# A transformer block on one core: expert biases kept in SBUF, the ends of both attentions reordered, table and result additions moved, unread projections added

## The chip, the cores and the metric

One core of a Trainium2 chip runs the whole program. The metric is the device time of one execution in microseconds (us), median of several. Before the change it is 1199.89 us (three runs, 1197.47 to 1200.57).

## The reference, cut to what matters

`x` has 16 x 256 tokens of width 128. Four residual parts follow each other, each with its layer norm ahead of it:

```python
x = x + attn_a(layernorm(x), ...)   # 16 heads, q/k/v mapped to latents of 32, rope on q and k, causal softmax
x = x + ffn(layernorm(x), ...)      # 8 experts, the best 2 of each token
x = x + attn_b(layernorm(x), ...)   # 16 heads of 8, causal softmax
x = x + ffn(layernorm(x), ...)      # the same experts again

def ffn(x):                         # flat: 4096 tokens
    logits = flat @ gate_w + gate_b
    topv, topi = top_k(logits, 2); topw = softmax(topv)
    out_e = gelu(flat @ w1[e] + b1[e]) @ w2[e] + b2[e]
    return sum over e of out_e * routing weight of e
```

## The kernel before, in words

All engines run one hand-written program each and meet by semaphores; nothing is reordered by a scheduler. The residual `X` (32 tiles of 128 tokens) stays in SBUF. Each attention goes over 8 chunks of 512 tokens, and each chunk over 8 units (two batch rows by four head groups), so 64 units. A table (`PlanA`, `Plan`) gives each unit a step or two of other work for bank 7 of PSUM: projections of the next chunk (`query`, `key`, `value`), and the closing of the chunk before (`turn`, `out_t`, `out`, `gate_t`, `gate`). What is left after unit 63 is `LAST`, here called the epilogue: it closes chunks 6 and 7 and, through `first_tiles`, starts on the first tiles of the experts.

In attention b a unit is a loop between two engines. TensorE turns the row maxima (L1744), VectorE joins them to the queries (`q_aug`, L1260), TensorE makes the scores of the next unit (L1905, L1908), VectorE takes their maxima (L954, L955). TensorE makes the unit's early projection (L1662 to L1664) while it waits for the join; in the last chunk there is no next chunk, so no early projection.

The expert stage routes 8192 pairs of token and expert into 39 tiles of 256 slots (`TILES`). The first half of the tokens is ranked and placed while the attention still runs. The second half is known only after the last gate, so the routing of it (`route_second`) runs on VectorE within the first tiles: ranks, slots, the one-hot factors `lane_hot` and `block_hot`, and then at tile `TABLE_AT` TensorE multiplies these into the table of which token stands in which slot (`tokens_of`, L1687), VectorE turns it into row numbers (`sources`), and sets `slots_ready` to 2. Tiles 0 to 8 (`EARLY` is 9) are gathered from the first table; from tile 9 on GpSimd's indirect DMAs (L621) wait for `slots_ready` 2. SyncE's load of the weights of tile 9 waits for it too, and behind that load in SyncE's queue stand the stores of results.

One tile i of the loop: TensorE turns the gathered rows of tile i+2 (`turn_rows`, L1767), makes the first product of tile i+1 (`up`, L1662 to L1664, 12 matmuls) and the second product of tile i (`down`, L1983, 16 matmuls). ScalarE copies the high half of the rows (L1436) and applies Gelu. VectorE makes the low half (`split_rows`, L1167) and adds the bias `b2` (`finish`, L1311). SyncE stores the result and loads weights four tiles ahead. `b2_rows`, 512 KB, is loaded anew before each expert stage by SyncE, after the attention has let go of its memory (`attended`), and VectorE waits for it (`bias_ready`) ahead of tile 2.

The results of finished tiles come back to tokens by other indirect DMAs (`got`, L730), 16 rings deep; VectorE adds them to X (L1376). A call adds one of 64 rows ("result"); the first 32 (`RESULTS`) need only tiles below 23. In the loop they are added three per tile from tile 28 on (`ADDED_AT`). In the first expert stage GpSimd gathers results 0 to 15, makes the root for chunk 0 of attention b, gathers 16 to 23, makes the root for chunk 1, gathers 24 to 31, and goes on to attention b. The other 32 results are added in attention b's chunks 1 to 6, and at the very end after the second stage.

## Time and profile before

| | |
|---|---|
| median of three runs | 1199.89 us |
| the profiled execution | 1191.1 us, its span 1189.4 us |
| TensorE busy | 1024.3 us (86%) |
| VectorE, ScalarE, GpSimd busy | 747.3, 648.2, 758.7 us |
| mean granted TensorE clock | 0.908 |

Stages in the profiled execution: attention a to 442, its epilogue and the first tiles to 477, expert stage 1 to 616.8, attention b to 963, its epilogue and first tiles to 1002, expert stage 2 to 1139, the last 32 results to 1184. A row of the timeline gives the start, the length, the engine, the line, what is written and read, and in brackets how long the engine sat idle before it and what released it. TensorE in attention a is close to full; the idle times are in the two epilogues, at the seams of the stages and at a few places in the expert stages.

### The profile page before, as it was taken

To read this page: it belongs to the slowest core of one execution; us is meant where nothing else is said; L and a number is where in the kernel's file an instruction comes from. 1 tells how busy PE (TensorE), PEld (TensorE's weight loads), DVE (VectorE), ACT (ScalarE), POOL (GpSimd) and SP (SyncE) were. 2 spreads that over 40 slices of the span, in tenths; PEclk is the share of its full clock that TensorE was granted. 3 is DMA by queue.
4 is the path that set the end of the run, shared out by engine and by line. 5 is a ranking of instruction groups with operands and counts; after the bars stand their busy time and mean duration, and the time that the engine had idled before them with its cause. 6 is when DMAs were issued, how large, how long until landed. Compare 5 with 4: busy or idle time off the path is not lost. (4 is left out here: it accounts for less than half of the span.)

```text
span 1189.4 us, 29763 instructions
## 1 busy us (share of the span) xinstructions
PE 1024.3 (86%) x11227; PEld 793.5 (67%) x11227; DVE 747.3 (63%) x1845; ACT 648.2 (55%) x1193; POOL 758.7 (64%) x824
## 2 busy tenths in 40 slices
PE   4799999999988987999877899999988878999820
PEld 3566776676765666999874556666655557999820
DVE  5878888888889954622345677777777626322332
ACT  1476777776755543455445667767755424455410
POOL 2788988888876746277663477667534233577765
PEclk9799999999998897999997999999988658999975
DMA  9100011010000023578940000000000024688732
GB/s 263 4 2 20 19 38 37 20 37 16 6 11 2 11 72 93 162 232 251 217 121 1 1 15 24 25 16 23 13 8 4 10 98 133 182 239 222 241 104 68
DMA packets 69805, 91.10 MB, mean 77 GB/s; under 512 B 15074, under 2 KB 49762, under 8 KB 69666
## 3 DMA queue, kind: packets, MB, share of 16 engines
q1 hardware_dynamic: 58226, 68.98, 18.4%
q0 software_dynamic: 9088, 18.63, 7.3%
q8 instruction: 93, 1.52, 0.6%
q10 hardware_dynamic: 2352, 1.58, 0.5%
q14 instruction: 46, 0.38, 0.1%
HBM read 68.45 MB, written 20.71 MB: 75 GB/s over the span
## 5 line engine op out<-in xcount | busy, mean ns | idle before, releaser
L1417 ACT ACTIVATE PT<-PS 128x768 f32<-128x768 f32 x256 | 207.1, 809 | 133.0 <-PE PS L1925 79.2
L608 POOL TENSOR_SCALAR_AFFINE_SELECT PT<-PT 128x512 f32<-128x512 f32 x256 | 179.4, 701 | 144.1 <-ACT PT L1417 143.5
L621 POOL DMA_INDIRECT xg<-normed,source x156 | 148.0, 949 | 94.8 <-DVE source L1101 48.1
L1448 ACT ACTIVATE hid<-PS,b_cols 128x256 f32<-128x256 f32 x312 | 122.5, 475 | 113.3 <-PE PS L1664 110.5
L1983 PE MATMUL PS<-W,hid 128*128 x1248 | 158.9, 283 | 0.1
L1983 PEld LDWEIGHTS PS<-W,hid 128*128 128x128 f32 x1248 | 152.6, 199 | 0.6 <-issue 0.5
L730 POOL DMA_INDIRECT got<-expert_rows,slot_of x128 | 122.7, 959 | 40.2 <-issue 34.4
L1311 DVE TENSOR_TENSOR y_rows<-PS,b_rows 128x256 f32<-128x256 f32 x78 | 33.1, 425 | 149.0 <-PE PS L1983 144.1
L1755 PE MATMUL PS<-PT,v_aug 128*32 128x256 f32 (+1 forms) x2048 | 117.9, 352 | 2.2 <-POOL PT L608 2.1
L1737 PE MATMUL PS<-causal_b,ident_b 128*128 128x256 bf16 x512 | 104.1, 287 | 13.5 <-DVE q_aug L1260 12.9
L1662 PE MATMUL PS<-xg_hi,w_ring 128*128 128x256 f32 x312 | 96.9, 311 | 16.7 <-DVE xg_lo L1167 13.0
L648 POOL TENSOR_TENSOR straight<-whole,C 128x512 f32<-128x512 f32 x64 | 83.7, 1308 | 14.5 <-ACT whole L1481 14.1
L1664 PE MATMUL PS<-xg_lo,w_ring 128*128 128x256 f32 x312 | 89.7, 288 | 0.0
L1663 PE MATMUL PS<-xg_hi,w_ring 128*128 128x256 f32 x312 | 89.7, 288 | 0.0
L963 DVE TENSOR_REDUCE M<-PS 128x2 f32<-128x512 f32 x128 | 87.1, 680 | 0.0
L1755 PEld LDWEIGHTS PS<-PT,v_aug 128*32 128x32 f32 x2048 | 56.0, 114 | 41.9 <-issue 11.3
L1744 PE MATMUL PS<-C,M 128*128 128x128 f32 x256 | 58.6, 312 | 26.6 <-DVE M L963 15.0
L962 DVE TENSOR_REDUCE M<-PS 128x2 f32<-128x256 f32 x128 | 54.0, 421 | 41.0 <-PE PS L1829 40.2
L1737 PEld LDWEIGHTS PS<-causal_b,ident_b 128*128 128x128 bf16 x512 | 41.4, 101 | 54.8 <-DVE q_aug L1260 29.0
L1376 DVE SCALAR_TENSOR_TENSOR X<-got,weight,X 128x128 f32<-128x128 f32 x128 | 45.6, 366 | 51.2 <-DMA got<-expert_rows,slot_of 49.5
L955 DVE TENSOR_REDUCE M<-PS 128x4 f32<-128x1024 f32 x64 | 77.8, 1215 | 0.0
L1662 PEld LDWEIGHTS PS<-xg_hi,w_ring 128*128 128x128 f32 x312 | 61.4, 197 | 18.8 <-DVE xg_lo L1167 15.1
(301 smaller groups left out, 2993.2 us busy)
## 6 DMA issues: line engine op xcount, KB each, us to landing
w_ring<-halves_w SPq DMA_DIRECT2D x78, 512.0 KB
expert_rows<-y_rows SPq DMA_DIRECT2D x78, 128.0 KB, 3.1
normed<-xn SPq DMA_DIRECT2D x16, 256.0 KB, 2.3
xg<-normed,source POOLq DMA_INDIRECT x156
W<-in_L_ffn_w_dram SPq DMA_DIRECT2D x1, 2048.0 KB, 13.8
halves_w<-w_hi SPq DMA_DIRECT2D x8, 256.0 KB, 2.3
halves_w<-W SPq DMA_DIRECT2D x8, 256.0 KB, 2.0
got<-expert_rows,slot_of POOLq DMA_INDIRECT x128, 2.7
```

The lines of the kernel that those rows point to most:

```text
L608: nc.gpsimd.affine_select(out=diagonals, in_=diagonals, pattern=[[0, 4], [1, P]], compare_op=ALU.is_ge, fill=0.0, base=0, channel_multipli ...
L621: nc.gpsimd.indirect_dma_start(out=xg[:, i % AHEAD, b_, :], out_offset=None, in_=normed if i >= EARLY else normed[0:NH * P, :], in_offset= ...
L730: nc.gpsimd.indirect_dma_start(out=got[:, at, :], out_offset=None, in_=rows_out if c >= RESULTS // (2 * CT) else rows_out[0:FIRST_DONE * R ...
L963: ins = v.tensor_reduce(M[:, 1, cols], PS[:, banks, P:3 * P], AX, ALU.max, negate=True)
L1417: s.activation(PT[:, unit % 2, pair, :, :, :], PS[:, 4:6, 0:3 * P].rearrange("p h (a q) -> p a h q", q=P), ACT.Exp).then_inc(m["exp_done"], 1)
L1448: ins = s.activation(hid[:, r % 2, k, :], h_bank[r % 2][k // 2][:, k % 2 * ROWS:(k % 2 + 1) * ROWS], ACT.Gelu, bias=b1_cols[:, bass.ds(e * ...
L1662: t_.matmul(o, w_hi, x_hi, start=start, stop=False, skip_group_check=True)
L1663: t_.matmul(o, w_lo, x_hi, start=False, stop=False, skip_group_check=True)
L1664: return t_.matmul(o, w_hi, x_lo, start=False, stop=True, skip_group_check=True)
L1737: t_.matmul(diagonal, ident_b[:, :], causal_b[:, :].unsqueeze(1).broadcast_to([P, 2, P]), start=True, stop=False, skip_group_check=True)
L1755: ins = t_.matmul(bank[6][j * L:(j + 1) * L, at + kb * P:at + S], v_aug[:, unit // UNITS % 2, 2 * b_ + kb, g * G + j, :], PT[:, unit % 2, ...
L1983: ins = t_.matmul(y_bank[r % 2][:, b_ * P:(b_ + 1) * P], hid[:, r % 2, k, b_ * P:(b_ + 1) * P], W2[:, bass.ds(e * F + k * D, D)], start=(k ...
```

## The change

Seven edits. The names of the parts are used in the prediction.

1. **Bias.** `b2_rows` gets memory of its own, is loaded once at the start behind the expert weights, and `attended` and `bias_ready` go.
2. **Epilogues.** `out_t` and `out` of chunk 7 now come ahead of `gate` of chunk 6, in both attentions. Tile 0 is turned after `out_t`, tile 1 after that `gate`, and tile 0's first product follows. ScalarE normalizes chunk 7 ahead of Gelu of tile 0.
3. **First tiles.** Tile 1's first product comes after tile 2's turn, tile 2's first product ahead of the ranks; `split_rows` of tile 2 moves into the last choice of experts.
4. **Table.** `TABLE_AT` is 6 instead of 5; the second table covers only blocks 18 to 77 (60 instead of 78 columns); its first 16 matmuls stand ahead of tile 6's second product, its last 16 behind it.
5. **Results.** They are added from tile 32 on, three per tile; the 11 left over (21 to 31) are added in the first four units of attention b, or after the loop in stage 2. The statistics of chunks 0 and 1 move from tiles 31 and 34 to tiles 34 and 37, and ScalarE normalizes chunk 0 one tile earlier.
6. **Unread projections.** In each unit of the last chunk of attention b TensorE makes a projection (three matmuls of 512 columns) into bank 7 that nobody reads.
7. Waits on `got_used` at units 2 and 6 of attention b.

The end of attention a and the first tiles, TensorE, before (L1712 is `turn`, L1698 `gate_t`, L1767 the turn of gathered rows, L1730 `gate`, L1716 `out_t`, L1720 `out`):

```order
L1712 MATMUL PS<-C,o_t 128x128 x4
L1698 MATMUL PS<-C,xn 128x128 x4
L1767 MATMUL PS<-C,xg 128x128 x2
L1730 MATMUL PS<-gate,gate_in 128x8 x4
L1716 MATMUL PS<-C,Y 128x128 x4
L1767 MATMUL PS<-C,xg 128x128 x2
L1720 MATMUL PS<-a_out_w,y_t 128x128 x4
L1662 MATMUL PS<-xg_hi,w_ring 128x256
```

And now:

```order
L1722 MATMUL PS<-C,o_t 128x128 x4
L1708 MATMUL PS<-C,xn 128x128 x4
L1726 MATMUL PS<-C,Y 128x128 x4
L1778 MATMUL PS<-C,xg 128x128 x2
L1730 MATMUL PS<-a_out_w,y_t 128x128 x4
L1741 MATMUL PS<-gate,gate_in 128x8 x4
L1778 MATMUL PS<-C,xg 128x128 x2
L1672 MATMUL PS<-xg_hi,w_ring 128x256
```

`out_t` (now L1726) moved ahead of tile 0's turn, and `gate` behind `out`.

The table in the expert loop, TensorE, before: it stands between tile 6's first product and tile 5's second (L1687, 78 columns):

```order
L1664 MATMUL PS<-xg_lo,w_ring 128x256
L1687 MATMUL PS<-block_hot,lane_hot 128x78 x32
L1974 TENSOR_LOAD expert_of
...
L1983 MATMUL PS<-W,hid 128x128 x5
L1767 MATMUL PS<-C,xg 128x128 x2
L1662 MATMUL PS<-xg_hi,w_ring 128x256
```

And now, between tile 7's first product and the turn of tile 9 (L1778):

```order
L1674 MATMUL PS<-xg_lo,w_ring 128x256
L1697 MATMUL PS<-block_hot,lane_hot 128x60 x16
L1991 TENSOR_LOAD expert_of
...
L2000 MATMUL PS<-W,hid 128x128 x5
L1697 MATMUL PS<-block_hot,lane_hot 128x60 x16
L1778 MATMUL PS<-C,xg 128x128 x2
```

The turn of tile 9 stood two second products, a turn and a first product behind the table; now it is the next instruction.

VectorE at the start of attention b's units, now (L1385 adds results, L1264 is the join, L954 and L955 the maxima); before, the four rows of L1385 were not there:

```order
L1264 TENSOR_TENSOR q_aug<-PS,qs 128x256
L918 SCALAR_TENSOR_TENSOR qs<-PS,b_bias,minus 128x512
L954 TENSOR_REDUCE M<-PS 128x4
L955 TENSOR_REDUCE M<-PS 128x4
L1385 SCALAR_TENSOR_TENSOR X<-got,weight,X 128x128 x3
L1264 TENSOR_TENSOR q_aug<-PS,qs 128x256
```

Each addition stands between the maxima of one unit and the join of the next. The diff, cut:

```diff
@@ -38,10 +38,10 @@
 FIRST_BLOCKS = FIRST_DONE * RB
-ADDED_AT = FIRST_DONE + 5
+ADDED_AT = FIRST_DONE + 9
 ADDS = 3
 RESULTS = 8 * CT
-TABLE_AT = 5
+TABLE_AT = 6
 SPLIT_AT = UNITS
@@ -161,7 +161,7 @@
     FIRST_CLOSE = [None, None, ("prep", 0, 1), None, ("value", 0, 1), None, ("prep", 0, 2), ("turn", 0, 0)]
-    LAST = [("turn", 1, 0, 7), ("gate_t", 0, -1, 0), ("gate", 0, -1, 1), ("out_t", 0, 0, 2), ("out", 0, 0, 3), ("gate_t", 0, 0, 4), ("gate", 0, 0, 5)]
+    LAST = [("turn", 1, 0, 7), ("gate_t", 0, -1, 0), ("out_t", 0, 0, 2), ("out", 0, 0, 3), ("gate", 0, -1, 1), ("gate_t", 0, 0, 4), ("gate", 0, 0, 5)]
@@ -295,8 +296,10 @@
     k = ADDS * (i - ADDED_AT)
-    end = RESULTS if i == TILES - 1 else min(k + ADDS, RESULTS)
-    return range(k, end) if i >= ADDED_AT else range(0)
+    return range(k, k + ADDS) if i >= ADDED_AT else range(0)
+ADDED = ADDS * (TILES - ADDED_AT)
@@ -531,6 +534,7 @@
             sp.dma_start(W2[:, :].rearrange("p (e k d) -> p e k d", e=E, k=FT), w2.rearrange("e (k p) d -> p e k d", p=P)).then_inc(experts_loaded, 16)
+            sp.dma_start(b2_rows[:, :, :].rearrange("p e d -> p (e d)"), b2.rearrange("e d -> (e d)").partition_broadcast(P)).then_inc(bias_loaded, 16)
             with nc.allow_non_contiguous_dma(reason="biases as columns"):
@@ -570,10 +574,6 @@
                     keep(c, gate_norm_b(c))
-                sp.wait_ge(attended[n], 1)
-                sp.dma_start(b2_rows[:, :, :].rearrange("p e d -> p (e d)"), b2.rearrange("e d -> (e d)").partition_broadcast(P)).then_inc(me["bias_ready"], 16)
@@ -1177,11 +1180,12 @@
                     closing(m, w, s, n == "a")
-                    if s.kind == "gate" and s.c == NCH - 2:
-                        split_rows(me, 0)
                     if s.kind == "out":
                         statistics(m, NCH - 1, 1 if n == "b" else 0)
+                    if s.kind == "gate" and s.c == NCH - 2:
+                        dve.wait_ge(m["freed_dve"], s.freed)
+                        split_rows(me, 0)
                         split_rows(me, 1)
@@ -1189,8 +1193,8 @@
                             choose(part, NT - CT, NT, me)
-                v.memset(scratch1[:, :], 0.0).then_inc(attended[n], 1)
-                dve.wait_ge(attended[n], 1)
+                            if part == 0:
+                                split_rows(me, 2)
@@ -1280,8 +1284,13 @@
                     if c == 0:
+                        if adds_at(unit):
+                            add_results("1", adds_at(unit))
                         if u == 2:
+                            dve.wait_ge(moe_sems["1"]["got_used"], 6 * CT)
                             statistics(m, 2)
+                        if u == 6:
+                            dve.wait_ge(moe_sems["1"]["got_used"], RESULTS)
                         if u == 7:
@@ -1349,13 +1358,13 @@
                     add_results(n, adds_in(i))
-                    if n == "1" and i == ADDED_AT + 3:
+                    if n == "1" and i == ADDED_AT + 2:
                         dve.wait_ge(m["got_used"], 2 * CT)
                         statistics(att_sems["b"], 0)
-                    if n == "1" and i == ADDED_AT + 6:
+                    if n == "1" and i == ADDED_AT + 5:
                         dve.wait_ge(m["got_used"], 4 * CT)
                         statistics(att_sems["b"], 1, 1)
-                dve.wait_ge(m["got_used"], RESULTS)
+                dve.wait_ge(m["got_used"], ADDED)
                 weigh(1, m)
@@ -1462,9 +1472,9 @@
                 s.activation(scratch3[:, :], C[0:1, 0:1], ACT.Gelu)
+                normal(n, st.c, gate_norm_b(st.c), st.c, range(CT), 1 if n == "b" else 0)
                 act.wait_ge(b1_loaded, 16)
                 gelu(me, 0)
-                normal(n, st.c, gate_norm_b(st.c), st.c, range(CT), 1 if n == "b" else 0)
@@ -1680,12 +1690,12 @@
-            def tokens_of(h, at):
-                for k in range(2):
-                    for t in range(NH):
-                        ins = t_.matmul(at, lane_hot[:, k, :, t], block_hot[:, k, 0:BLOCKS if h else FIRST_BLOCKS, t], start=(k + t == 0),
-                                        stop=(k == 1 and t == NH - 1), skip_group_check=True)
+            def tokens_of(h, at, k, tiles=range(NH)):
+                blocks = slice(EARLY * RB, BLOCKS) if h else slice(0, FIRST_BLOCKS)
+                for t in tiles:
+                    ins = t_.matmul(at, lane_hot[:, k, :, t], block_hot[:, k, blocks, t], start=(k + t == 0),
+                                    stop=(k == 1 and t == NH - 1), skip_group_check=True)
                 return ins
@@ -1782,15 +1793,13 @@
-                if (s.kind, s.c) == ("gate_t", NCH - 2):
+                if s.kind == "out_t":
                     pe.wait_ge(m["slots_ready"], 1)
                     turn_rows(m, 0)
-                elif s.kind == "out_t":
+                elif (s.kind, s.c) == ("gate", NCH - 2):
                     turn_rows(m, 1)
-                elif s.kind == "out":
                     pe.wait_ge(experts_loaded, 32)
                     up(m, 0)
-                    up(m, 1)
@@ -1932,6 +1941,12 @@
+                def unread(last):
+                    pe.wait_ge(m["freed_act" if last.by_act else "freed_dve"], last.freed)
+                    product(bank[7], w["hi"][0][:, 0:P], w["lo"][0][:, 0:P], x_hi[:, 1, :], x_lo[:, 1, :])
                 causal(range(4))
@@ -1946,6 +1961,8 @@
                         step(plan.early[unit])
+                    elif unit >= end - UNITS:
+                        unread(next(s for u in range(unit - 1, 0, -1) for s in (plan.extra[u], plan.late[u], plan.early[u]) if s))
                     if unit + 1 < end:
@@ -1984,21 +2001,29 @@
+                table = y_bank[(TABLE_AT + 1) % 2][:, EARLY * RB:BLOCKS]
                 for i in range(TILES):
                         turn_rows(m, i + 2)
-                    if 0 < i < TILES - 1:
+                    if i == 0:
+                        up(m, 1)
+                        down(0)
+                        up(m, 2)
+                        pe.wait_ge(m["mask_ready"], 2)
+                        ranks(1, y_bank[1]).then_inc(m["rank_ready"], 1)
+                        continue
+                    if 1 < i < TILES - 1:
                         up(m, i + 1)
                         pe.wait_ge(m["y_ready"], i)
-                        tokens_of(1, y_bank[(i + 1) % 2][:, 0:BLOCKS]).then_inc(m["table_ready"], 1)
+                        tokens_of(1, table, 0)
                     if i == TABLE_AT + 1:
                     down(i)
-                    if i == 0:
-                        pe.wait_ge(m["mask_ready"], 2)
-                        ranks(1, y_bank[1]).then_inc(m["rank_ready"], 1)
+                    if i == TABLE_AT:
+                        pe.wait_ge(m["hots_ready"], 3)
+                        tokens_of(1, table, 1).then_inc(m["table_ready"], 1)
```

## Rows read from the trace of the kernel before

**Rows 1.** Part 2 of the page: granted clock in 40 slices
```profile
PEclk9799999999998897999997999999988658999975
```

**Rows 2.** Timeline of VectorE, both epilogues: start, length, what, idle before and releaser
```profile
472.26 0.42 DVE L1167 TENSOR_TENSOR xg_lo<-PS,xg_hi 128x256 fp32r<-128x256 f32 x1 [3.82 <-issue]
995.67 0.42 DVE L1167 TENSOR_TENSOR xg_lo<-PS,xg_hi 128x256 fp32r<-128x256 f32 x1 [4.07 <-issue]
```

**Rows 3.** The same, queue of SyncE (issues; length is until the queue takes them)
```profile
468.50 0.35 SPq L576 DMA_DIRECT2D b_rows<-in_L_ffn_b_dram  x1
```

**Rows 4.** The same, TensorE, first tiles of both expert stages
```profile
472.73 0.38 PE L1662 MATMUL PS<-xg_hi,w_ring 128*128 128x256 f32 x1 [3.21 <-DVE xg_lo L1167]
477.74 0.36 PE L1662 MATMUL PS<-xg_hi,w_ring 128*128 128x256 f32 x1
973.84 0.66 PE L1767 MATMUL PS<-C,xg 128*128 128x128 f32 x2 [3.78 <-DMA xg<-normed,source]
996.15 0.58 PE L1662 MATMUL PS<-xg_hi,w_ring 128*128 128x256 f32 x1 [3.30 <-DVE xg_lo L1167]
```

**Rows 5.** Table of tokens, to the first row gathered by it: TensorE, GpSimd, TensorE
```profile
955.54 3.15 PE L1687 MATMUL PS<-block_hot,lane_hot 128*128 128x46 f16 x32
489.88 5.00 PE L1687 MATMUL PS<-block_hot,lane_hot 128*128 128x78 f16 x32
496.63 0.95 POOL L621 DMA_INDIRECT xg<-normed,source  x1 [23.69 <-DVE source L1101]
497.88 0.95 POOL L621 DMA_INDIRECT xg<-normed,source  x1 [0.31 <-issue]
501.74 0.44 PE L1767 MATMUL PS<-C,xg 128*128 128x128 f32 x2 [0.54 <-DMA xg<-normed,source]
1025.80 0.38 PE L1767 MATMUL PS<-C,xg 128*128 128x128 f32 x2
```

**Rows 6.** Waits within the expert stages: TensorE
```profile
580.79 0.35 PE L1662 MATMUL PS<-xg_hi,w_ring 128*128 128x256 f32 x1 [3.51 <-issue]
608.00 0.39 PE L1662 MATMUL PS<-xg_hi,w_ring 128*128 128x256 f32 x1 [1.78 <-DVE xg_lo L1167]
1107.93 0.55 PE L1662 MATMUL PS<-xg_hi,w_ring 128*128 128x256 f32 x1 [3.24 <-DVE xg_lo L1167]
```

**Rows 7.** What VectorE waited for there
```profile
583.16 0.35 DVE L1376 SCALAR_TENSOR_TENSOR X<-got,weight,X 128x128 f32<-128x128 f32 x1 [5.46 <-DMA got<-expert_rows,slot_of]
1105.12 0.35 DVE L1376 SCALAR_TENSOR_TENSOR X<-got,weight,X 128x128 f32<-128x128 f32 x1 [3.42 <-DMA got<-expert_rows,slot_of]
```

**Rows 8.** Between expert stage 1 and attention b: TensorE, VectorE, GpSimd
```profile
612.75 4.05 PE L1983 MATMUL PS<-W,hid 128*128 x32
607.46 0.16 DVE L792 TENSOR_SCALAR var_eps<-mv 128x4 f32<-128x4 f32 x1
609.19 1.02 POOL L730 DMA_INDIRECT got<-expert_rows,slot_of  x1 [0.16 <-DVE X L1376]
621.93 0.69 DVE L904 TENSOR_TENSOR x_lo<-PS,x_hi 128x512 fp32r<-128x512 f32 x1
627.17 1.26 POOL L697 TENSOR_TENSOR ks<-whole,minus 128x512 fp32r<-128x512 f32 x1 [8.20 <-ACT minus L1556]
```

**Rows 9.** TensorE, unit 2 of attention b
```profile
653.74 0.39 PE L1737 MATMUL PS<-causal_b,ident_b 128*128 128x256 bf16 x2 [0.77 <-DVE q_aug L1260]
```

**Rows 10.** Windows: length, busy (count) by engine, granted clock, DMA share, GB/s
```profile
868.00:909.00 41.00, 35.71 (x348) 24.08 (x348) 29.11 (x69) 22.27 (x34) 15.35 (x20) 0.88 0.03 8
912.00:940.00 28.00, 25.08 (x199) 14.86 (x200) 18.31 (x39) 10.18 (x17) 9.83 (x13) 0.53 0.04 11
948.00:960.00 12.00, 9.89 (x87) 7.84 (x88) 5.71 (x16) 2.44 (x3) 1.91 (x3) 0.62 0.01 2
580.00:584.00 4.00, 3.21 (x28) 3.24 (x29) 0.65 (x2) 1.43 (x4) 2.92 (x4) 1.00 0.87 312
1107.00:1111.00 4.00, 3.07 (x14) 3.07 (x15) 2.34 (x7) 0.04 (x1) 2.93 (x4) 0.62 0.80 265
```

54 lines of the change are left out of this document (30 added, 24 removed).

## The prediction

> **What bounds the kernel now.** I read the clock by slices first [rows 1]: TensorE is at full clock through most of the kernel and at half only at the ends of the attentions and in the last tenth. So the change, which touches only seams, can act only at seams. Then, seam by seam, the timelines of the engines [rows 2 to 9], and last a table of windows [rows 10]. Seen there:
>
> - Between the attentions and the experts VectorE stands still for 3.82 and 4.07 us ahead of the low half of tile 2 [rows 2]. The profile says "issue", so no engine releases it; what it waits for is the bias load, issued at 468.50 [rows 3]. TensorE behind it waits 3.21 and 3.30 us [rows 4].
> - In the end of attention b TensorE also waits 3.78 us for the gathered rows of tile 0 (973.84), with `out_t`, `gate` and `out` queued behind [rows 4].
> - In the middle of the expert stages TensorE waits 3.51, 1.78 and 3.24 us [rows 6]. Two of these come from VectorE, which waits for results to come back (5.46 and 3.42 us, [rows 7]).
> - From expert stage 1 to attention b, the last second product ends at 616.8, but `x_lo` starts at 621.93 and GpSimd's first `ks` at 627.17 [rows 8].
> - The last chunk of attention b runs at a granted clock of 0.53, its neighbour at 0.88 [rows 10].
>
> A tile of the experts takes 3.41 us: from the turn of tile 9 at 1025.80 to the end of the turn of tile 32 (1107.93 less the wait of 3.24, less 0.38) are 78.5 us for 23 tiles [rows 5, 6].
>
> **The change part by part.** Sums are for the profiled execution, 1191.1 us.
>
> *Bias, epilogues, first tiles.* The product of tile 3 starts at 477.74 in stage 1 [rows 4]. Without the bias wait it is 3.21 earlier. Further, tile 2's product now runs while VectorE still chooses experts, and the ranks follow; then VectorE's copy and layout (about 3 us) ends while TensorE does one second product. Walking through the queues I get 473.5: **-4.2** (bounds -3.2 and -5). What is late next there is VectorE's layout of the second half. In stage 2 the wait for the rows of tile 0 is partly filled, since `out_t` (1.1 us) and ScalarE's copy behind it now run within it: 3.30 for the bias and, with half the wait left standing for the `out` behind it, some 2.2 of the 3.78: **-5.5** (bounds -3.3 and -7.1, both waits whole). The bias load itself moves behind 4 MB of expert weights at the start; nobody waits on it before 460, so 0. SyncE loses the wait and loads the weights of tile 4 earlier; they were not late.
>
> *Table.* This is where I expect the gain to go. Before, the table begins at 489.88 and tile 9 is turned at 501.74, 11.86 later, after a wait of only 0.54, because tile 5's and 6's second products and tile 7's first stand between [rows 5]. The chain behind the table does not get shorter: it ends at 494.88, VectorE's `sources`, GpSimd's first two gathers (496.63 and 497.88), landing, turn at 501.74: 6.86 us. Now the table begins one tile later (+3.41), takes the width of 60 columns: 3.15 us at 46 and 5.00 at 78 give 3.97 by the line between them, and has tile 6's second product in its middle, 2.0 (4.05 for two, [rows 8]), so 6.0 to its end; and the turn of tile 9 is TensorE's next instruction. So 3.41 + 6.0 + 6.86 = 16.3 instead of 11.86: +4.4, and I add 0.3 for a lower clock in the middle. TensorE stands some 6.7 us there, and everything of the stage is queued behind. What the wait does to the clock: after a wait of 3.24 us the next 4 us were granted 0.62, after one of 3.51 they were granted 1.00 [rows 6, 10]. A product and a second product at half clock cost some 1.6 us more (12 matmuls from 1107.93 at 0.55 for one instead of 0.35). With a wait twice as long I take the loss: **+6.3 per stage** (bounds +4.4 and +8).
>
> The Trainium skill, "TensorE: Matmul & The Clock Gate", section "HAM oscillation — how this bites in real kernels", says that a wait for a DMA between groups of matmuls makes the next group start at half clock. By that rule the 1.6 us are paid in both stages; by the row of 580 to 584 they might be spared, and the sum would be 3.2 lower. The trace of before shows both answers once.
>
> At tile 9 the stages thus stand at -4.2 + 6.3 = **+2.1** and -5.5 + 6.3 = **+0.8**.
>
> *Results from tile 32.* VectorE no longer waits at tile 28, since the first results are by then long there. In stage 1 the wait of 3.51 is "issue", not VectorE; the weights of tile 30 come late, and stay late (0). What goes is 1.78 and some 0.85 at tile 31: **-2.6** (bounds -1.8 and -6.1). In stage 2 the 3.24 and its clock loss of 1.2 go, but the next weights were issued in the same jam as the results, so I take **-2.5** (bounds 0 and -4.5).
>
> *The seam to attention b.* Here two things pull apart. VectorE is done earlier: `x_lo` at about 620.4 instead of 621.93. But the statistics of chunk 1 move to tile 37, 1.0 us behind the last product instead of 9.3 ahead of it (607.46, [rows 8]), and GpSimd gathers results 24 to 31 only after the root of that chunk: 1.7 us (607.46 to 609.19) and 8 gathers at 1.25 us [rows 5, 8] end 12.7 us behind, with `ks` right behind them, where before it started 627.17 - 616.8 = 10.4 behind. TensorE's first scores and the other projections wait for that `ks`: **+2.1** net (bounds -1.5, if the earlier `x_lo` decided, and +3).
>
> *Eleven results in units 0 to 3.* Each costs 0.35 us [rows 7], 1.06 for three, between maxima and join. Units with an early projection hide it; unit 2 has none, and the join of unit 3, late already by 0.77 [rows 9], comes 1.06 later: with a little at unit 1 **+1.5** (bounds 0 and +4).
>
> *Unread projections.* Eight times three matmuls of 512 columns, in time that TensorE waits for the join. They pay by the clock: in 912 to 940 VectorE is busy 18.31 of 28 us; in chunk 6 it is busy 29.11 of 41, 71% [rows 10]. At that share the same work takes 25.8, 2.2 less; in 948 to 960 5.71/0.71 gives 8.0 of 12, of which I count 2.3, since the table's 3.15 us [rows 5] are in it at any clock. **-4.5** (bounds +4, all of them beyond the waits at half clock, and -8).
>
> *The end.* After the last product GpSimd's 32 gathers at 1.25 us set the pace; the 11 results added there take 4 us in VectorE's shadow: 0.
>
> Sum: +2.1 + 0.8 - 2.6 - 2.5 + 2.1 + 1.5 - 4.5 = -3.1. The execution would take 1188 us; the runs shown stand 8.8 higher (1199.89 against 1191.1), so the forecast is 1199.9 - 3.1 = **1196.8**.
>
> **The rivals.**
> (A) *The table's wait is short.* If the chain to tile 9 is covered, by a landing faster than 2.9 us and no loss of clock, the stages keep their start: -3.1 - 2 x 4.5 = -12, 1188. For it: in stage 2 the turn at 1025.80 had no wait at all. Against it: GpSimd issues the second gather 3 us behind the table whatever lands.
> (B) *The clock does not rise.* The unread projections do not bring the clock back and lengthen each unit by what exceeds the wait: 1.4 us at half clock less 0.5 to 1, so +4 instead of -4.5: +5.4, 1205. It decides as soon as TensorE, not the join, ends last in those units. Against it: in 868 to 909 real projections of the same size went with 0.88. For it: the clock fell even there.
> (C) *The clock rises at once and stays through the epilogue*: -8 instead of -4.5 and two us less behind it: -8.6, 1191.
> (D) *Nothing gained in the middle*: late weights keep the waits of the expert stages [rows 6] where they are: -3.1 + 5.1 = +2, 1202.
>
> **How the numbers follow.** Forecast 0.38, A 0.13, B 0.14, C 0.22, D 0.13. A measurement of this kernel can tell some 0.3%, 3.6 us, from no change; the forecast itself lies near that bound, within a spread of 4 us, so I give it 0.17 faster, 0.17 same, 0.04 slower. A and C count as faster, B as slower, D as same with a third slower. Faster 0.52, same 0.26, slower 0.22. Range: 1187 (just inside A) to 1204 (most of B); the likeliest case's own is 1192 to 1200.
>
> **What would show each step.** Right: no idle time of VectorE ahead of tile 2's low half and tile 3's first product 4 to 6 us earlier against the end of attention; TensorE waiting 6 to 7 us ahead of the turn of tile 9, released by the gather, with GpSimd's wait on `source` as long as now; no wait of VectorE for results in either stage; `ks` 12 to 13 us behind the last second product of stage 1, with GpSimd busy until then; a granted clock above 0.8 from 912 to 960. Wrong: a wait at tile 9 below 4 us; `ks` within 10 us; a clock near 0.5 in the last chunk, or units there longer than now.

## The result and the profile after

The changed kernel takes 1203.23 us, the median of its runs (1194.1 to 1210.83); the kernel before took 1197.4 in the runs beside it (1186.79 to 1204.82). The ratio is 1.0058, 95% interval 1.0037 to 1.0079: about 7 us slower, where 3 us faster was forecast. The profiled execution has a span of 1197.1 us against 1189.4. Every ratio below leaves out executions more than 1.5% above the fastest of their kernel as slow; beside four of the experiments (table at tile 6 alone, results from tile 30, tile 1's product back, results alone) that takes away 13 of the 29 of the kernel before, and since the ratios of medians of all executions are 0.2 to 0.6% lower there, these medians stand beside them.

Part 2 of the page of the changed kernel, granted clock in 40 slices; slices counted from 0. Against [rows 1] slices 1, 15 and 16 (449 to 509 us) and slice 22 (658 to 688, the first chunk of attention b) are lower, and those of the last chunk and the epilogue behind it (31 to 33) are higher:

```profile
PEclk9699999999998896899997799999988869899975
```

The same milestones in both traces show where the 7.7 us went. First the rows that [rows 4, 5, 8] do not have. Of the kernel before: joins of units 8, 56 and 63 (VectorE), last turn of attention a's and of attention b's epilogue, tile 3's product in stage 2, last second product (TensorE):

```profile
680.07 0.41 DVE L1260 TENSOR_TENSOR q_aug<-PS,qs 128x256 fp32r<-128x256 f32 x1
916.98 0.42 DVE L1260 TENSOR_TENSOR q_aug<-PS,qs 128x256 fp32r<-128x256 f32 x1
959.18 0.42 DVE L1260 TENSOR_TENSOR q_aug<-PS,qs 128x256 fp32r<-128x256 f32 x1
448.35 1.09 PE L1712 MATMUL PS<-C,o_t 128*128 128x128 f32 x4 [0.81 <-ACT o_t L1422]
967.50 0.87 PE L1712 MATMUL PS<-C,o_t 128*128 128x128 f32 x3 [0.81 <-ACT o_t L1422]
1002.38 0.36 PE L1662 MATMUL PS<-xg_hi,w_ring 128*128 128x256 f32 x1
1134.69 4.12 PE L1983 MATMUL PS<-W,hid 128*128 x32
```

Of the changed kernel, timeline of TensorE: last turn, tile 3's product and tile 9's turn in stage 1, last second product; then the first scores; then the same four of stage 2; then VectorE's joins of units 8, 56 and 63:

```profile
449.97 1.09 PE L1722 MATMUL PS<-C,o_t 128*128 128x128 f32 x4 [0.81 <-ACT o_t L1432]
479.01 0.38 PE L1672 MATMUL PS<-xg_hi,w_ring 128*128 128x256 f32 x1 [1.97 <-DVE xg_lo L1170]
507.48 0.69 PE L1778 MATMUL PS<-C,xg 128*128 128x128 f32 x2 [6.97 <-DMA xg<-normed,source]
618.53 4.06 PE L2000 MATMUL PS<-W,hid 128*128 x32
637.85 0.48 PE L1914 MATMUL PS<-ks,qs 32*128 32x128 f32 x4 [8.38 <-POOL ks L697]
973.64 0.66 PE L1722 MATMUL PS<-C,o_t 128*128 128x128 f32 x2 [0.81 <-ACT o_t L1432]
1004.38 0.38 PE L1672 MATMUL PS<-xg_hi,w_ring 128*128 128x256 f32 x1 [1.69 <-DVE xg_lo L1170]
1034.00 0.69 PE L1778 MATMUL PS<-C,xg 128*128 128x128 f32 x2 [8.04 <-DMA xg<-normed,source]
1142.28 4.05 PE L2000 MATMUL PS<-W,hid 128*128 x32
...
693.85 0.41 DVE L1264 TENSOR_TENSOR q_aug<-PS,qs 128x256 fp32r<-128x256 f32 x1
928.25 0.42 DVE L1264 TENSOR_TENSOR q_aug<-PS,qs 128x256 fp32r<-128x256 f32 x1
965.58 0.42 DVE L1264 TENSOR_TENSOR q_aug<-PS,qs 128x256 fp32r<-128x256 f32 x1
```

| stretch | before | after | change | forecast |
|---|---|---|---|---|
| start to last turn of attention a | 448.35 | 449.97 | +1.6 | 0 |
| to tile 3's product, stage 1 | 29.39 | 29.04 | -0.4 | -4.2 |
| to tile 9's turn | 24.00 | 28.47 | +4.5 | +4.7 |
| to the end of the last second product | 115.06 | 115.11 | 0.0 | +1.6 - 2.6 |
| to the join of unit 8 | 63.3 | 71.3 | +8.0 | +2.1 + 1.5 |
| units 8 to 56 | 236.9 | 234.4 | -2.5 | 0 |
| units 56 to 63 | 42.2 | 37.3 | -4.9 | -4.5 |
| to the last turn of attention b | 8.3 | 8.1 | -0.3 | 0 |
| to tile 3's product, stage 2 | 34.88 | 30.74 | -4.1 | -5.5 |
| to tile 9's turn | 23.42 | 29.62 | +6.2 | +4.7 |
| to the end of the last second product | 113.0 | 112.3 | -0.7 | +1.6 - 2.5 |
| to the end | 50.6 | 50.8 | +0.2 | 0 |

A stretch "to the end of the last second product" is called the middle of its stage. Two rows are no effect of the change as far as the runs tell: attention a's last turn lies between 444.5 and 451.9 us in most of the traces below, in kernels whose attention a is the same (two have it at 455 and 463), and units 8 to 56 (233.8 to 237.4 us) are the same code too. A single trace can thus be off by some us in such a stretch; verdicts go by the ratios, and by stretches where many traces agree. Forecast and trace differ by 10.8 us in all. The stretch to unit 8 has 4.4 of them and tile 3 in stage 1 has 3.8; the two middles have 1.2, tile 3 and tile 9 in stage 2 have 1.4 and 1.5.

### The profile page after: what moved, and what is told of

Same layout as the page of the kernel before. It is cut to its first block, busy times and chain, and to the rows that moved or that the text cites. A ratio compares the mean times of both kernels' runs of the same rounds, so it can differ in the third digit from the quotient of the medians.

```text
span 1197.1 us, 29813 instructions
## 1 busy us (share of the span) xinstructions
PE 1025.5 (86%) x11251; PEld 794.3 (66%) x11251; DVE 745.8 (62%) x1843; ACT 648.0 (54%) x1193; POOL 760.0 (63%) x824
## 4 chain that ended last, share of the span: by engine, by line
PE 65%; DVE 20%; ACT 4%; POOL 4%; issue 4%; DMA 2%; SPq 0%; DVEq 0%; POOLq 0%; ACTq 0%
PE PS L2000 11%; PE PS L1672 8%; PE PS L1674 6%; PE PS L1673 6%; PE PS L1832 5%; PE PS L1766 5%; PE PS L1748 3%; POOL got L730 3%; DVE M L955 3%; PE PS L1755 3%; PE PS L1812 2%; DVE M L963 2%; PE PS L1778 1%; ACT minus L1566 1%; DVE M L954 1%
## 5 line engine op out<-in xcount | busy, mean ns | idle before, releaser
L2000 PE MATMUL PS<-W,hid 128*128 x1248 | 156.0, 279 | 1.1 <-DVE mark L1329 1.0
L2000 PEld LDWEIGHTS PS<-W,hid 128*128 128x128 f32 x1248 | 150.0, 196 | 1.9 <-issue 1.9
L730 POOL DMA_INDIRECT got<-expert_rows,slot_of x128 | 122.7, 959 | 41.2 <-issue 26.3
L1766 PE MATMUL PS<-PT,v_aug 128*32 128x256 f32 (+1 forms) x2048 | 115.5, 346 | 1.8 <-POOL PT L608 1.8
L1748 PE MATMUL PS<-causal_b,ident_b 128*128 128x256 bf16 x512 | 103.1, 285 | 11.2 <-DVE q_aug L1264 10.7
L955 DVE TENSOR_REDUCE M<-PS 128x4 f32<-128x1024 f32 x64 | 77.9, 1216 | 0.0
L954 DVE TENSOR_REDUCE M<-PS 128x4 f32<-128x512 f32 x64 | 44.1, 689 | 45.6 <-PE PS L1917 45.6
L1672 PEld LDWEIGHTS PS<-xg_hi,w_ring 128*128 128x128 f32 x312 | 62.3, 200 | 13.8 <-issue 8.5
```

Source lines behind the costliest of these rows:

```text
L730: nc.gpsimd.indirect_dma_start(out=got[:, at, :], out_offset=None, in_=rows_out if c >= RESULTS // (2 * CT) else rows_out[0:FIRST_DONE * R ...
L955: v.tensor_reduce(M[:, 1, first::L], PS[:, 0:4, P:3 * P], AX, ALU.max, negate=True).then_inc(m["max_ready"], 1)
L1672: t_.matmul(o, w_hi, x_hi, start=start, stop=False, skip_group_check=True)
L1748: t_.matmul(diagonal, ident_b[:, :], causal_b[:, :].unsqueeze(1).broadcast_to([P, 2, P]), start=True, stop=False, skip_group_check=True)
L1766: ins = t_.matmul(bank[6][j * L:(j + 1) * L, at + kb * P:at + S], v_aug[:, unit // UNITS % 2, 2 * b_ + kb, g * G + j, :], PT[:, unit % 2, ...
L2000: ins = t_.matmul(y_bank[r % 2][:, b_ * P:(b_ + 1) * P], hid[:, r % 2, k, b_ * P:(b_ + 1) * P], W2[:, bass.ds(e * F + k * D, D)], start=(k ...
```

## The experiments

Ratios are to the kernel before in the runs beside each kernel, with 95% intervals. The first four undo one part of the change, or do one alone.

**Table back at tile 5.**

```diff
-TABLE_AT = 6
+TABLE_AT = 5
-                        pe.wait_ge(m["hots_ready"], 2)
+                        pe.wait_ge(m["hots_ready"], 3)
                         tokens_of(1, table, 0)
+                        tokens_of(1, table, 1).then_inc(m["table_ready"], 1)
...
-                    if i == TABLE_AT:
-                        pe.wait_ge(m["hots_ready"], 3)
-                        tokens_of(1, table, 1).then_inc(m["table_ready"], 1)
```

> The changed kernel with one part undone: the second table stands again at tile 5, whole and ahead of tile 5's second product (60 columns as in the change). Theory T (the wait at tile 9 is the chain of the late table, and it costs its own length and the half clock behind it): the waits of 6.97 and 8.04 us ahead of the turn of tile 9 fall below 1 us, the 6 us behind them run at full clock, and the kernel takes 10 to 12 us less than the changed one, a ratio of 0.996 to 0.998 to the kernel before. Rival W (the expert stages are paced by the expert weights and the rows, so time won at tile 9 is given back as waits between tiles 25 and 33): the waits at tile 9 go as well, but those around 584 and 1113 us grow by as much as 5 us each, and the kernel takes only 2 to 5 us less, a ratio of 1.002 to 1.004.

Measured: 1184.26 us, ratio 0.9898 (0.9851 to 0.9946), some 19 us less than the whole change. Timeline of TensorE, turns of tile 9:

```profile
497.73 0.69 PE L1778 MATMUL PS<-C,xg 128*128 128x128 f32 x2 [2.33 <-DMA xg<-normed,source]
1023.09 0.38 PE L1778 MATMUL PS<-C,xg 128*128 128x128 f32 x2
```

From tile 3 to tile 9 it is 24.9 and 23.0 us, about as before the change (24.0 and 23.4). By its ratio the table is the dearest part, and stage 2 shows rival W wrong: its 163.0 us from the last turn to the last product are 9.7 less than in the changed kernel. In stage 1 the sum is only 0.9 less (171.7 against 172.6), as rival W has it: one wait of 2.33 remained, with a clock of 0.72 over the six us behind it, and the middle took 3.4 us more. The trace thus shows 10.6 of the 19 us in the stages.

**Results as before.** In the changed kernel ADDED_AT is FIRST_DONE + 5 again, all 32 results are added in the stage, the statistics stand 3 and 6 tiles behind the start, and nothing is added in units 0 to 3.

> The changed kernel with one part undone: results are added from tile 28 on, all 32 of them within the stage, with the statistics of chunks 0 and 1 at tiles 31 and 34 and ScalarE's normalization of chunk 0 one tile later, as before the change; nothing is added in units 0 to 3. Theory T (the late statistics of chunk 1 hold GpSimd's gathers of results 24 to 31, and ks stands behind them; the additions delay the first units): ks starts about 10.4 us behind the last second product instead of 13.8, and attention b's first chunk is 2 us shorter; the waits for results in the middle of the stages come back and take 3 us in stage 1 and 1 in stage 2, so that the kernel takes about 1.5 us less than the changed one, a ratio near 1.0045 to the kernel before. Rival W (those waits were set by the expert weights, not by results): they stay as they are, and the kernel takes 5 to 6 us less than the changed one, a ratio of 1.001.

Measured: 1195.07 us, ratio 0.9992 (0.9959 to 1.0026): 8 us less, more than either theory. `ks` starts 10.7 us behind the last product (GpSimd, 636.28, after a wait of 8.19 for ScalarE's half), and unit 8's join stands 65.9 behind it instead of 71.3. In the trace the stages take 3.4 and 1.0 us more than in the changed kernel, as theory T says, so that it shows only 1 us of the 8.

**No unread projections.** The call of `unread` is taken out.

> The changed kernel without the unread projections in the last chunk of attention b. Theory T (they pay by the clock): the granted clock from the start of that chunk on falls back to about 0.5, the stretch to the last turn is 5.3 us longer, and the ratio to the kernel before is about 1.010. Rival C (the clock in that chunk differs from one execution to the next, and the extra work changes nothing): the ratio stays at 1.006.

Measured: 1205.95 us, ratio 1.0101 (1.0066 to 1.0135), as theory T has it. Units 56 to 63 take 42.4 us instead of 37.3, and rival C is out, since all traces fall in two groups (table at the end of this section). Windows of the last chunk, in the changed kernel and in this one, at the place of the second of [rows 10] (same columns):

```profile
923.46:951.46 28.00, 25.77 (x250) 16.17 (x251) 19.95 (x42) 11.83 (x19) 11.39 (x15) 0.82 0.04 11
```

```profile
924.30:952.30 28.00, 24.49 (x201) 14.71 (x202) 17.91 (x39) 10.54 (x17) 9.88 (x13) 0.58 0.04 11
```

There are 49 more matmuls in the same time, 15 of them unread, and the granted clock is 0.82 instead of 0.58.

**Bias alone, on the kernel before.** `b2_rows` has memory of its own, is loaded once, and `attended` and `bias_ready` are gone.

> The kernel before with one part of the change alone: the expert biases have memory of their own and are loaded once at the start, and the waits on them at the start of both expert stages are gone. Theory T (the bias waits of 3.21 and 3.30 us are time on the path): tile 2's first product starts 3 us earlier in both stages, and the kernel takes 6 us less than before, a ratio of 0.995. Rival K (the clock takes it back: without those waits the product still runs at half clock, or VectorE's chain of choices and layout ends last there): less than 3 us, a ratio of 0.998. Rival S (the load at the start delays the prologue by about 1.5 us, as the changed kernel's trace shows attention a 1.6 us late): 1.5 us more in either case.

Measured: 1187.57 us, ratio 0.9943 (0.991 to 0.9976): 6.8 us faster. Tile 3's product stands 26.21 us behind the last turn in stage 1 and 32.13 in stage 2, 3.2 and 2.8 earlier than before:

```profile
477.33 0.39 PE L1658 MATMUL PS<-xg_hi,w_ring 128*128 128x256 f32 x1 [1.25 <-DVE xg_lo L1165]
998.77 0.38 PE L1658 MATMUL PS<-xg_hi,w_ring 128*128 128x256 f32 x1 [0.85 <-DVE xg_lo L1165]
```

That is theory T. Rival S's 1.5 us can't be read from one trace, since attention a varies by more.

The next four ask whether these parts add, and what they consist of.

**Table and results both undone.** The first two edits together.

> The changed kernel with two parts undone together: the table back at tile 5, whole, and the results and statistics timed as before the change. Left of the change are the kept bias, the reordered epilogues and first tiles, the narrower table and the unread projections. Theory T (the two costs stand in different places and add): ratios of 0.990 and 0.999 alone, against 1.006 for the whole change, give 0.983 together. Rival W (in stage 1 the expert weights pace the middle, so what is won at tile 9 comes back as waits behind it; in the traces so far stage 1 took 168.5 to 175.5 us whatever was done): 0.988 to 0.990.

Measured: 1177.66 us, ratio 0.9861 (0.9818 to 0.9905). It beats both kernels. The point lies between the two theories, and its interval touches both.

**ks ahead of the last eight gathers.**

```diff
                 for c in range(RESULTS // (2 * CT)):
+                    if n == "1" and c == 3:
+                        for r in range(4):
+                            pool.wait_ge(m[f"stored{r}"], 16 * len(range(r, TILES, 4)))
+                        first_keys()
                     gather_results(n, c)
```

The diff is cut: `first_keys` makes the `ks` that stood at the head of attention b's program on GpSimd, and there they are taken out.

> The changed kernel, but GpSimd makes the first ks of attention b ahead of the gathers of results 24 to 31 instead of behind them; nothing is added or left out. Theory T (ks stands behind eight gathers of 1.25 us): ks starts when ScalarE's halves are ready, some 8 us behind the last second product instead of 13.8, the first scores follow, and the kernel takes 4 to 5 us less than the changed one, a ratio of 1.002. Rival G (the eight gathers then stand in the first units, ahead of GpSimd's masks, and the additions of units 1 to 3 wait for their landing): the time comes back within the first three units and the ratio stays at 1.005 to 1.008.

Measured: 1203.12 us, ratio 1.0073 (1.0043 to 1.0103). Rival G. Timeline of GpSimd: the first `ks`, 9.2 us behind the last product, and the first mask of unit 0 (AFFINE_SELECT) with the next `ks`:

```profile
631.84 1.26 POOL L724 TENSOR_TENSOR ks<-whole,minus 128x512 fp32r<-128x512 f32 x1 [5.71 <-ACT minus L1576]
...
649.58 0.64 POOL L608 TENSOR_SCALAR_AFFINE_SELECT PT<-PT 128x512 f32<-128x512 f32 x1
650.20 1.26 POOL L697 TENSOR_TENSOR ks<-whole,minus 128x512 fp32r<-128x512 f32 x1
```

The first scores come 4.65 us earlier (10.6 behind the last product instead of 15.3), but unit 8's join is at 71.4, as in the changed kernel (71.3). The ten us of gathers cost the same ahead of `ks` and behind it.

**Table at tile 6, but whole.** In the changed kernel both halves stand ahead of tile 6's second product.

> The changed kernel with one piece undone: the second table is not split around tile 6's second product but stands whole ahead of it, still at tile 6. Theory T (the wait ahead of tile 9 is the chain behind the table, and the split puts 2.0 us of it into that chain): the wait falls from 7 to 8 us to about 5 to 6, 2 us per stage are gone, a ratio of 1.0025. The rest of the 19 us by which the table at tile 5 is faster than the change is then the delay by one tile. Rival S (the second product behind the table is only swapped against the wait, and rows of tile 9 arrive by the chain of GpSimd alone): less than 1 us, 1.005.

Measured: 1200.77 us, ratio 1.0042 (1.0013 to 1.0071). The waits ahead of tile 9 are 4.44 and 5.10 us instead of 6.97 and 8.04, slightly below theory T's 5 to 6; the time falls by 2 us instead of 4, and the intervals allow both, and nothing as well. The split is the small half of the table's price.

**Bias and unread projections alone, on the kernel before.**

> The kernel before with two parts of the change alone: the kept bias and the unread projections. Theory T (the parts add): 0.9943 for the bias alone less 0.0043 for the unread projections, a ratio of 0.990. Against the run of the changed kernel with table and results undone it also prices what is left between the two, the reordered epilogues and first tiles and the 18 columns less in the table: if the reordering pays the 3 us forecast for it (1 in stage 1, 2.2 in stage 2), that kernel is faster than this one by 0.0025 or more; if TensorE only stays at half clock for longer in it, as the changed kernel's trace of stage 1 shows from 459 to 471 us, the two are equal or this one is the faster.

Measured: 1182.91 us, ratio 0.9894 (0.9861 to 0.9926): the parts add. The kernel with the reordering as well (0.9861) is 4 us faster by the two ratios, but the intervals overlap, and a gain of 4 us is as possible as none.

Four more take single sizes.

**Table at tile 6 alone, on the kernel before.** TABLE_AT is 6, nothing else.

> The kernel before with one size changed: TABLE_AT is 6 instead of 5; the table is whole, 78 columns wide and ahead of tile 6's second product. Theory D (the delay by one tile alone is what the table costs: in pairs of kernels that differ in it the ratios are 1.004 against 0.990, and 0.999 against 0.986): a wait of 4 to 6 us ahead of tile 9 in both stages, half clock behind it, and a ratio of 1.010 to 1.014. Rival P (the prediction's sizes, 4.4 us per stage for delay and split, of which the split has 2.0): 5 us in all, a ratio of 1.004, and the rest of those differences belongs to the other parts it met there.

Measured: 1204.83 us, ratio 1.009 (1.0053 to 1.0128), 11 us slower (7.8 by the medians of all, 1204.83 against 1197.01), with waits of 5.23 and 4.41 us ahead of tile 9. That is nearer to theory D than to rival P's 1.004. In the trace the stages are 7.5 and 3.8 us longer from the last turn to the last product than before the change. Here the delay alone costs less than the 16 to 17 us by which the pairs with and without it differ (0.9898 against 1.0042, 0.9861 against 0.9992, the second with the split); each of those differences is uncertain by some 6 us.

**Results from tile 30.**

```diff
-ADDED_AT = FIRST_DONE + 9
+ADDED_AT = FIRST_DONE + 7
```

> The changed kernel with one size changed: results are added from tile 30 on instead of 32 (27 in the stage, 5 in the first two units; statistics at tiles 32 and 35). Theory R (the gather of result k into the ring of 16 must wait for the addition of result k-16, so the additions set when GpSimd gets through its 32 gathers): GpSimd ends them about 6.8 us earlier, ks starts some 10.4 us behind the last second product instead of 13.8, and with fewer additions in the units the kernel takes 4 to 5 us less than the changed one, a ratio of 1.002. Rival M (what is won there comes back as waits of VectorE for results in the middle of the stages): ratio 1.005 or more.

Measured: 1192.61 us, ratio 0.9992 (0.9956 to 1.0028), the same as with results from tile 28 (by the medians of all 4.4 us below the kernel before, 1197.01). Timeline of GpSimd, its last gather and `ks`:

```profile
628.81 0.94 POOL L730 DMA_INDIRECT got<-expert_rows,slot_of  x1 [0.30 <-issue]
632.07 1.26 POOL L697 TENSOR_TENSOR ks<-whole,minus 128x512 fp32r<-128x512 f32 x1 [2.32 <-ACT minus L1566]
```

GpSimd is 2.32 us idle ahead of `ks`, 8.6 us behind the last product, so the gathers no longer hold it, and unit 8's join stands 62.0 us behind the last product instead of 71.3. Theory R. By the ratios all of the loss lies in the last two tiles of delay.

**Tile 1's first product back.** To table and results undone, one piece of the first tiles: `up(m, 1)` stands behind `up(m, 0)` in `first_tiles` again.

> The kernel with table and results undone (ratio 0.986), and one piece of the epilogue's reordering undone too: tile 1's first product stands again right behind tile 0's instead of behind the ranks' turn. Theory C (in the new order TensorE has only one product between two waits there, and its clock stays at half for 10 us longer in stage 1, which eats the 4.2 us forecast): the granted clock is 1.00 again from about 12 us behind the last turn of attention a, tile 3's product starts 3 to 4 us earlier in stage 1 and 1 to 2 in stage 2, ratio 0.983 to 0.984. Rival W (stage 1 gives back whatever comes early, as waits for expert weights near tile 28; stage 2 was at full clock there in any case): ratio 0.986, with tile 3 earlier and the wait near tile 28 longer.

Measured: 1179.24 us, ratio 0.9873 (0.9817 to 0.9929), or 0.9852 by the medians of all. Last turn and tile 3's product in both stages:

```profile
462.98 1.08 PE L1722 MATMUL PS<-C,o_t 128*128 128x128 f32 x4 [0.81 <-ACT o_t L1432]
489.19 0.38 PE L1672 MATMUL PS<-xg_hi,w_ring 128*128 128x256 f32 x1 [2.07 <-DVE xg_lo L1170]
972.74 0.66 PE L1722 MATMUL PS<-C,o_t 128*128 128x128 f32 x2 [0.81 <-ACT o_t L1432]
1001.79 0.38 PE L1672 MATMUL PS<-xg_hi,w_ring 128*128 128x256 f32 x1 [1.85 <-DVE xg_lo L1170]
```

26.21 and 29.05 us, where the kernel it is made from has 29.04 and 30.77: theory C's first half. The windows of five us, 17 us behind the last turn (same columns as [rows 10]), of this kernel and of the changed one (the kernel it is made from has 0.53 over five us at the same place):

```profile
479.60:484.60 5.00, 4.59 (x49) 4.10 (x48) 3.44 (x20) 2.15 (x6) 3.78 (x5) 1.00 0.19 57
```

```profile
466.60:471.60 5.00, 5.00 (x27) 5.00 (x27) 2.63 (x15) 1.94 (x5) 3.78 (x5) 0.54 0.21 53
```

With two first products in a row the clock is 1.00 there, with one between two waits 0.54. The total did not move with it: the ratio is that of the kernel it is made from, so either the later waits took the 4.5 us or they are within the spread; this run can't say which. It can't say either how much of the 2.8 us in stage 1 is the clock and how much the gap ahead of `gate` that tile 1's product fills again (a wait of 1.49 us in the changed kernel, of 0.78 in this one).

**Results alone, on the kernel before.**

> The kernel before with one part of the change alone: results from tile 32 on, the 11 left over in the first four units of attention b or behind the loop, the statistics and ScalarE's normalization moved with them. Theory R (the late additions push GpSimd's gathers into the seam, 3.5 us there and 2 in the first units, and the waits in the middle that they were to remove were half those of late weights): slower by 5 to 8 us, a ratio of 1.004 to 1.007. Rival P (the prediction's terms: 2.6 and 2.5 won in the stages, 2.1 and 1.5 lost behind them): 1.5 us faster, a ratio of 0.999.

Measured: 1199.92 us, ratio 1.0082 (1.0046 to 1.0118), 9.8 us slower and theory R with a little more; by the medians of all, 1199.92 against 1197.01, it is 2.9 us slower, which alone would not shut out rival P. The trace decides: TensorE waits 7.20 us for `ks`, and unit 8's join stands at 71.8 instead of 63.3. In stage 1 the wait that the profile calls "issue" is there as ever, 4.66 us at 591.29, and from tile 9 to the last product it is 116.7 against 115.1 us; in stage 2 the same stretch is 3.5 us shorter.

The results were now the open cause, so two more were run.

**No additions in unit 2.** They stand in units 0, 1, 3 and 4.

> The changed kernel, but the eleven results left over are added in units 0, 1, 3 and 4 of attention b instead of 0 to 3; nothing else is moved. In the changed kernel's trace three additions (1.44 us) stand ahead of the statistics in unit 2, the join of unit 3 comes 7.8 us behind that of unit 2 instead of 6.9, TensorE waits 2.12 us, and the 10 us behind it were granted 0.50. Theory U (that wait and the clock behind it are most of what the first units cost beyond the seam): the wait falls below 1 us, the clock stays near 0.9, unit 8's join comes 67 to 68 us behind the last second product instead of 71.3, and the kernel takes 3 to 4 us less than the changed one, a ratio of 1.002 to 1.003. Rival S (what the first units lose is set by GpSimd's late ks and masks, wherever the additions stand): unit 8's join stays at 70 or more, ratio 1.005 to 1.008.

Measured: 1200.63 us, ratio 1.002 (0.9987 to 1.0053), theory U's number; its interval and that of the changed kernel (1.0037 to 1.0079) overlap. In the trace the wait is gone:

```profile
667.77 0.39 PE L1750 MATMUL PS<-causal_b,ident_b 128*128 128x256 bf16 x2 [0.76 <-DVE q_aug L1266]
```

But unit 8's join is at 68.5, 2.8 us earlier and not 3 to 4, and the clock was half elsewhere: 0.71 from 645.5 to 665.5, where the changed kernel had 0.95 from 644.3 to 664.3. Rival S's 70 is not reached, but most of the 8 us stays.

**Table at tile 5, results from tile 30.**

> The changed kernel with the table back at tile 5, whole, and results from tile 30 on (two tiles later than before the change, two earlier than in it). Theory R (up to tile 30 GpSimd's gathers still end ahead of ks, and later additions spare VectorE's waits for results in the stages): at least as fast as with results from tile 28, a ratio of 0.983 to 0.986. Rival M (the waits for results that it spares are replaced by waits for expert weights, and five additions stand in the first units): 0.986 to 0.990.

Measured: 1182.78 us, ratio 0.9863 (0.9824 to 0.9902). It is the third kernel between 0.986 and 0.988; between them, and between theory R and rival M, nothing is decided. What they share, the kept bias, the unread projections, the epilogues' new order and the narrower table at tile 5, makes the kernel 16 us faster than before.

**The same stretches in all sixteen traces.** Each range covers all kernels of its group, whatever else they change, in us, with their number:

| stretch | part | with it | without it |
|---|---|---|---|
| last turn to last product, stage 1 | table at tile 6 | 172.6 to 177.6 (8) | 165.6 to 171.7 (8) |
| last turn to last product, stage 2 | table at tile 6 | 170.2 to 175.1 (8) | 162.9 to 171.3 (8) |
| last product to unit 8's join | results from tile 32, against 28 | 68.5 to 73.4 (7) | 61.8 to 67.7 (7) |
| units 56 to 63 | unread projections | 35.6 to 37.4 (11) | 42.2 to 42.4 (5) |
| last turn to tile 3, stage 1, bias kept | tile 1's product moved away | 28.3 to 30.0 (10) | 26.0 to 26.2 (3) |


## Why the prediction was wrong

**Results from tile 32: the step that failed.** The prediction put it as "the first results are by then long there", -2.6 and -2.5, with +2.1 for the seam and +1.5 for the units, 1.5 us faster in all. It costs 3 to 10 us: by the ratios 9.8 alone (2.9 by the medians of all), 8 when undone in the changed kernel, 4.4 when undone with the table at tile 5 (0.9898 against 0.9861). In the traces of these three pairs unit 8's join comes 8.5, 5.4 and 5.7 us later behind the last product, where 3.6 was forecast, and the two stages together give 1.0 and 4.4 and lose 0.7, where 5.1 was to be won. So the part is 4 to 11 us beside its forecast, somewhere between under half of the miss of 10 and all of it; in the trace of the changed kernel the stretch to unit 8 and the middles have 5.6 of 10.8. Three things were missed.

First, a gather of result k goes into a ring of 16 and waits for the addition of result k-16 (`got_used`). Adding later thus also gathers later; the prediction saw GpSimd's order, but took its time from the statistics alone. Timeline of GpSimd in the changed kernel (L600 is the root of a chunk's variance, L730 a gather):

```profile
613.52 1.05 POOL L600 TENSOR_TENSOR rstd<-var_eps,neg_half 128x4 f32<-128x4 f32 x1 [16.60 <-DVE var_eps L792]
...
624.12 0.94 POOL L730 DMA_INDIRECT got<-expert_rows,slot_of  x1 [0.30 <-issue]
625.08 1.11 POOL L600 TENSOR_TENSOR rstd<-var_eps,neg_half 128x4 f32<-128x4 f32 x1
...
635.46 0.94 POOL L730 DMA_INDIRECT got<-expert_rows,slot_of  x1 [0.30 <-issue]
636.42 1.28 POOL L697 TENSOR_TENSOR ks<-whole,minus 128x512 fp32r<-128x512 f32 x1
```

It idles 16.60 us in the stage and then runs without a pause, sixteen gathers, until `ks`, 13.8 us behind the last product (forecast 12.7, [rows 8] give 10.4). Started two tiles earlier it has the pause ahead of `ks` (the run from tile 30). That the order can't repair it, the run with `ks` first shows.

Second, the additions in the units. The forecast gave unit 2 the 1.06 us of three additions. They took 1.44, and TensorE, the clock included, lost more. The changed kernel, VectorE's additions and join, then TensorE, then the ten us behind it:

```profile
659.74 1.44 DVE L1385 SCALAR_TENSOR_TENSOR X<-got,weight,X 128x128 f32<-128x128 f32 x3
662.55 0.42 DVE L1264 TENSOR_TENSOR q_aug<-PS,qs 128x256 fp32r<-128x256 f32 x1
```

```profile
663.02 0.61 PE L1748 MATMUL PS<-causal_b,ident_b 128*128 128x256 bf16 x2 [2.12 <-DVE q_aug L1264]
```

```profile
664.30:674.30 10.00, 10.00 (x70) 5.76 (x65) 5.15 (x8) 6.38 (x11) 3.13 (x4) 0.50 0.00 0
```

So the units cost 4.5 us (8.0 less the seam's 3.5) instead of 1.5. Without additions in unit 2 some 2.8 of them are gone; what makes up the rest was not separated.

Third, in stage 1 there was nothing to win. The wait of 1.78 us did go: one of 1.5 to 1.9 us stands there in all seven traces with results from tile 28 and in none with later ones. But from tile 9 to the last product it is 115.1 to 118.4 us in those seven and 115.1 to 118.5 in the seven with results from tile 32. All of them have a wait of 2.2 to 5.6 us near tile 28 that the profile calls "issue"; the prediction had read it as late weights and left it out of the sum, which is argued, not shown. Rival D said as much, at 1202, and the time lies near it, but by luck: it explains the 5 us that were not won in the stages, not those lost behind them, and other parts missed too.

**Epilogues and first tiles: half right.** Forecast -4.2 and -5.5, in the trace -0.4 and -4.1. The bias was priced rightly (3.2 and 2.8 of 3.21 and 3.30 [rows 4]). What failed, and it is the second step, is that moving tile 1's first product away is free: in stage 1 a gap is left open, the clock stays at half until 471, and all that the bias gave is lost (29.04 against 26.21 with the bias alone). With that product back the two stages show -3.2 and -5.8, close to the forecast.

**Table: right.** The wait was forecast at some 6.7 and is 6.97 and 8.04; the turn stands 4.5 and 6.2 later behind tile 3, where 4.7 was forecast. The price of half clock, 1.6 a stage, was low, but near: the six us behind the wait were granted 0.61 and 0.68, which is 2.3 and 1.9 us (an estimate: the length times what is missing from 1.00):

```profile
507.48:513.48 6.00, 6.00 (x34) 6.00 (x35) 0.42 (x1) 1.95 (x5) 4.48 (x6) 0.61 0.59 212
1034.00:1040.00 6.00, 6.00 (x37) 6.00 (x38) 0.83 (x3) 2.32 (x6) 4.61 (x5) 0.68 0.53 178
```

Forecast 12.6 in all; measured 10.8 for the delay alone and about 2 for the split, or 19 when undone in the changed kernel (both uncertain by 4 to 7). In the traces of the four pairs that differ in the table both stages together, from the last turn to the last product, differ by 10.6, 11.3, 15.7 and 16.3 us. Rival A is dead. Of the two answers that the prediction left open for the clock, half clock came in both stages. The Trainium skill ("TensorE: Matmul & The Clock Gate", "HAM oscillation — how this bites in real kernels") says that the group of matmuls behind a wait for a DMA starts at half clock; behind these two waits for gathered rows it did. Behind a shorter wait, which the profile calls "issue", it did not: this row of the changed kernel starts behind 2.23 us and has the length of full clock, 0.36, and the ten us from 1113 were granted 1.00.

```profile
1113.51 0.36 PE L1672 MATMUL PS<-xg_hi,w_ring 128*128 128x256 f32 x1 [2.23 <-issue]
```

**Unread projections: right.** Forecast -4.5; -4.9 in the trace, 5.1 by the ratio when taken out (1.0101 against 1.0058), 5.9 when added to the bias. Rivals B and C are out: the clock rises, though not at once and not to the end (0.76 and 0.73 from 920 to 940, 1.00 to 960, then 0.75 to the last join).

**The sum.** Terms by ratios of single changes: bias -6.8, unread -5 to -6, table +11 and split +2, results +3 to +10, reordering -4 to +1. They add to -1 to 12, and 7 was measured. The forecast had the same list with -1.5 at the results.

## What to carry to other kernels

When work is moved to a later place, follow what it frees as well as what it needs: here an addition frees a ring slot, so moving additions made sixteen gathers some 12 us later, ten of them behind the last product, at a seam where the same engine makes the first keys. A gain at one seam is worth as little as the next wait behind it; undoing one part at a time found within a change that is 7 us slower a kernel that is 16 us faster than before. In this kernel, where TensorE's clock was at half, work that nobody reads paid, and a product moved out of a gap cost what the removed wait had won.

## What the runs showed of the hardware that was not expected

- A stretch of half clock follows small things. A wait of 2.12 us was followed by ten us at 0.50, one of 2.23 us by ten at 1.00, both in the same execution. In the ten us up to the first wait TensorE had been busy 7.79, up to the second 10.00, both at 1.00.
- One first product between two waits of 1.06 and 1.49 us left the clock at 0.54 until 471; two in a row brought it to 1.00 some 7 us sooner in the run with tile 1's product back.
- The order of eight gathers against `ks` moved the first scores by 4.65 us and the join of unit 8 by 0.1: GpSimd's 1.25 us per gather is paid once its queue is full, wherever it stands.
- Stage 1 takes between 165.6 and 177.6 us from the last turn to the last product over all these kernels. The table splits them, with tile 5 below 172 and tile 6 above; what spreads each group by 5 to 6 us was not settled. A wait of 2.2 to 5.6 us near tile 28 is in all of them.
